# Storing the turned context once and loading it back, in a gated two-layer block on one core

## The reference

```
x = x + tanh(g_xattn[0]) * L0_xattn(layernorm(x), ctx, ctx, Wq, bq, ...)
x = x + tanh(g_ffn[0])   * L0_ffn(layernorm(x), controller, f1, f2, bias)
x = x + tanh(g_xattn[1]) * L1_xattn(layernorm(x), ctx, ctx, mask)
x = x + tanh(g_ffn[1])   * L1_ffn(layernorm(x), ln_g, ln_b, w1, w2)
# L0_xattn: 16 heads of 32; a query sees itself and every 32nd key
#   k = ctx @ Wk + bk; v = ctx @ Wv + bv; q = x @ Wq + bq; softmax(q k^T / sqrt(32)) v @ Wo + bo
# L0_ffn: in each group of 16 tokens, 64 slots each pick the token with the
#   largest logit; relu(sel @ f1 + bias) @ f2 is added back to the picked token
# L1_xattn: one head of width 512, no projections
logits = einsum('bqd,bkd->bqk', q, k) * 512**-0.5 + mask * -1e9
out    = einsum('bqk,bkd->bqd', softmax(logits), v)        # k = v = ctx
# L1_ffn: layernorm, int8 activations (scale from a 0.995 quantile), ternary weights, gelu
```

## Time and profile before

| | |
|---|---|
| median of three runs | 2006.31 us (2002.03 to 2006.43) |
| profiled execution | 2007.47 us, its span 2005.9 us |
| busy of the span | PE 1554.9, DVE 1184.0, PEld 1038.0, ACT 900.8, POOL 413.3 us |
| first stage, `phase1` | 23 to 662 us |
| `phase2a` | 663.6 to 873.1 us |
| joint stage, `phase2b3` | 873.9 to 1348.1 us |
| rest | 1349.2 us to the end |
| DMA | 167.08 MB, 83 GB/s over the span |

### The profile page before, as it was taken

One profiled execution on the slowest core, in us unless ns is written; L12 is line 12 of the kernel. 1 busy time (PEld: TensorE's weight loads), 2 busy tenths in 40 slices (PEclk: granted clock), 3 DMA queues, 4 the chain that ended last, 5 costly groups with the idle time before them and its releaser, 6 DMA issues. The chain is left out here.

```text
span 2005.9 us, 30396 instructions
## 1 busy us (share of the span) xinstructions
PE 1554.9 (78%) x10558; PEld 1038.0 (52%) x10558; DVE 1184.0 (59%) x2707; ACT 900.8 (45%) x1582; POOL 413.3 (21%) x411
## 2 busy tenths in 40 slices
PE   3999999999996488838999999931145991299996
PEld 3777767777774477714555555531133441134442
DVE  4576676666664344303676666755665896555552
ACT  2333333323322255523555555533066663477772
POOL 0232232232232100011455554450000000000000
PEclk9999999999998699968999999975566995599998
DMA  4112212211211832264233333218000000012221
GB/s 150 64 55 75 86 54 75 85 54 75 85 39 54 282 115 95 85 215 141 90 111 111 99 110 111 80 64 326 0 2 2 1 0 2 0 43 85 84 84 45
DMA packets 80829, 167.08 MB, mean 83 GB/s; under 512 B 14064, under 2 KB 25680, under 8 KB 79696
## 3 DMA queue, kind: packets, MB, share of 16 engines
q1 hardware_dynamic: 76304, 148.90, 21.3%
q0 software_dynamic: 4416, 16.78, 2.5%
HBM read 110.34 MB, written 55.31 MB: 83 GB/s over the span
## 5 line engine op out<-in xcount | busy, mean ns | idle before, releaser
L1892 PE MATMUL p_z<-qT,w1T 128*128 (+1 forms) x1024 | 246.8, 386 | 8.5 <-PEq L113 6.0
L1892 PEld LDWEIGHTS p_z<-qT,w1T 128*128 128x128 bf16 x1024 | 100.5, 99 | 137.1 <-issue 14.5
L1378 DVE TENSOR_TENSOR p_il<-p_f,p_ih 128x512 fp32r<-128x512 f32 x128 | 88.5, 692 | 129.6 <-ACT p_ih L1214 129.1
L1214 ACT ACTIVATE p_ih<-p_f 128x512 fp32r<-128x512 f32 x128 | 76.5, 598 | 152.5 <-PE p_f L1090 152.5
L1090 PE MATMUL p_f<-p_f2s,p_z 128*32 128x512 f32 x1024 | 137.6, 611 | 1.0 <-DMA p_z<-inner_d 0.6
L2202 PE MATMUL p_o<-w2T,p_Gq 128*128 128x512 bf16 x512 | 128.7, 381 | 2.2 <-DVE p_Gq L2270 2.2
L943 DVE COPY p_selT<-p_sel 128x512 f32<-128x512 f32 x64 | 66.8, 1046 | 96.0 <-PE p_sel L850 96.0
L850 PE MATMUL p_sel<-p_pick,p_xp 128*128 128x128 bf16 (+1 forms) x1536 | 97.2, 229 | 31.9 <-ACT p_selT L899 18.7
L2288 DVE TENSOR_SCALAR p_r<-p_g,p_s 128x512 f32<-128x512 f32 x128 | 62.2, 486 | 90.7 <-ACT p_g L2228 90.6
L850 PEld LDWEIGHTS p_sel<-p_pick,p_xp 128*128 128x128 bf16 x1536 | 94.0, 103 | 38.1 <-issue 29.7
L1949 DVE MAX8 p_tops<-hid 128x8 f32<-128x128 f32 x512 | 99.6, 278 | 23.0 <-ACT hid L1933 23.0
(11 more groups left out here) (302 smaller groups left out, 4055.3 us busy)
## 6 DMA issues: line engine op xcount, KB each, us to landing
p_cin<-in_ctx_dram SPq DMA_DIRECT2D x32, 512.0 KB, 4.6
xparts<-p_parts SPq DMA_DIRECT2D x16, 768.0 KB, 3.3
p_xp<-xparts SPq DMA_DIRECT2D x4, 3072.0 KB, 24.4
p_xin<-in_x_dram SPq DMA_DIRECT2D x16, 512.0 KB, 4.4
residual<-p_x SPq DMA_DIRECT2D x16, 512.0 KB, 3.2
p_f<-in_L_ffn_f_dram POOLq DMA_DIRECT2D x16, 512.0 KB, 4.3
inner_d<-p_inner POOLq DMA_DIRECT2D x4, 2048.0 KB, 9.4
p_z<-inner_d SPq DMA_DIRECT2D x16, 512.0 KB, 3.7
```

The costliest lines, as they stand in the source:

```text
L1214: act.activation(ih[m % ID][:, :], bf[m % FD][:, :], ACT.Copy).then_inc(s["hi_done"], 1)
L1378: dve.tensor_tensor(il[m % ID][:, :], bf[m % FD][:, :], ih[m % ID][:, :].bitcast(F32), ALU.subtract).then_inc(s["lo_done"], 1)
L1892: mm = pe.matmul(bank, w1T[:, c, fc * P:(fc + 1) * P], qT[:, c, bass.ds(first, TB)], start=(c == 0), stop=(c == C - 1))
```

## The change

The first stage gets a DRAM tensor `ctxT` of 16 batches x 2 parts x 512 KB. In each step SP, after the loads of the next batch, waits for DVE's low part (`ctxT` semaphore), and stores both parts; before ACT writes the buffer again for the next batch it waits for the stores (`ctxT_out`). At the end SP waits for all of them.

In the joint stage `turn_ctx`, the two `turned_highs` and the two `turned_lows` of the context go. POOL issues two loads per batch into the same buffers, after `rstd2` and before `values_low`, once `S_full` says that the scores of the batch before have read them. `scores` waits for `cT_in` in place of `c_low`; `turn_xn` takes over the wait on the bank that `turn_ctx` had; SP's reload of `cin` no longer waits for `cT_full`.

```diff
@@ phase1, block.sync, step @@
                 if F:
+                    sp.wait_ge(s["ctxT"], n.next(s["ctxT"], NT))
+                    n.apart()
+                    for k in range(2):
+                        sp.dma_start(ctxT_d[b, k], ctxT[k][:, :, :].bitcast(F32)).then_inc(s["ctxT_out"], 16)
 
                     sp.wait_ge(s["V_done"], n.next(s["V_done"], NT))
...
             sp.wait_ge(s["perm_out"], 16 * B)
+            sp.wait_ge(s["ctxT_out"], 32 * B)
@@ phase1, block.scalar, step @@
                 if F:
+                    if (used := n.reuse(s["ctxT_out"], 1, 32)) is not None:
+                        act.wait_ge(s["ctxT_out"], used)
                     for t in range(NT):
                         high(ctxT, t, "ctx_high")
@@ phase2b3, block.sync @@
                 if i >= 2 and live(i):
-                    sp.wait_ge(s["cT_full"], NT * (i - 1))
                     sp.wait_ge(s["v_low"], i - 1)
                     load_ctx(i)
@@ phase2b3, block.tensor @@
-            def turn_ctx(b):
-                pe.wait_ge(s[f"c_in{b % 2}"], 16 * (b // 2 + 1))
-                for t in range(NT):
-
-                    if b + 2 < B:
-                        pe.wait_ge(s["permT_done"], NT * (b + 2) + t + 1)
-                    else:
-                        pe.wait_ge(s["n_low"], NT * (b - 1) + t + 1)
-                    turn_tile(bT[t], cin[b % 2][:, t, :], s["cT_full"])
-
             def turn_xn(b):
                 for t in range(NT):
                     pe.wait_ge(s["norm1"], NT * b + t + 1)
-                    pe.wait_ge(s["c_low"], NT * b + t + 1)
+
+                    if b + 2 < B:
+                        pe.wait_ge(s["permT_done"], NT * (b + 2) + t + 1)
+                    elif b >= 1:
+                        pe.wait_ge(s["n_low"], NT * (b - 1) + t + 1)
                     turn_tile(bT[t], xn[:, t, :], s["nT_full"])
 
             def scores(b, t):
                 if t == 0:
-                    pe.wait_ge(s["c_low"], NT * (b + 1))
+                    pe.wait_ge(s["cT_in"], 32 * (b + 1))
                     pe.wait_ge(s["n_low"], NT * (b + 1))
...
-                    if k == 3 and live(i - 1):
-                        turn_ctx(i - 1)
@@ phase2b3, block.scalar @@
-                    if k == 3 and live(i - 1):
-                        turned_highs(i - 1, ctxT, s["cT_full"], s["c_high"])
@@ phase2b3, block.gpsimd @@
+            def load_ctxT(b):
+                if b >= 1:
+                    pool.wait_ge(s["S_full"], b)
+                for k in range(2):
+                    pool.dma_start(ctxT[k][:, :, :], ctxT_d[b, k].bitcast(F32R)).then_inc(s["cT_in"], 16)
...
                 if live(i - 3):
                     rstd2(i - 3)
+                if live(i - 1):
+                    load_ctxT(i - 1)
                 if live(i - 2):
                     values_low(i - 2)
@@ phase2b3, block.vector @@
-                    if k == 4 and live(i - 1):
-                        turned_lows(i - 1, ctxT, s["c_high"], s["c_low"])
```

More of the change, by code:

```diff
@@ L138, in shape_constants, with phase1 @@
     }
-def phase1(nc, x, ctx, gx, Wq, bq, Wk, bk, Wv, bv, Wo, bo, ctrl, K, x_mid, xparts, perm_d, vg_d):
+def phase1(nc, x, ctx, gx, Wq, bq, Wk, bk, Wv, bv, Wo, bo, ctrl, K, x_mid, xparts, perm_d, vg_d, ctxT_d):
     xt = x.rearrange("b (t p) d -> b p t d", p=P)
@@ L257, in phase1 @@
             vg_out vrep_in vbd_done x1_out var2 rstd2 norm2 b0_done r1_done b1_done b2_done parts_out
-            logits_full logits_taken pmT_done aside_sp aside_pe aside_dve""".split()
+            logits_full logits_taken pmT_done ctxT_out aside_sp aside_pe aside_dve""".split()
         s = es.enter_context(semaphores(nc, "p1_", names))
@@ L956, with phase2b3 @@
 NC1 = TILES * D // SEG * 8
-def phase2b3(nc, inner_d, perm_d, f2, gf, x_mid, ctx, mask, gx, ln_g, ln_b, K, x3_d, hid_d, cand):
+def phase2b3(nc, inner_d, perm_d, f2, gf, x_mid, ctx, ctxT_d, mask, gx, ln_g, ln_b, K, x3_d, hid_d, cand):
     FD, ID, ZD, XD, LAG = 2, 3, 2, 4, 2
@@ L996, in phase2b3 @@
         names = """const_in ln_in identb_done tanh_done spread_zero spread_done turned permT_done f_full hi_done lo_done scattered added
-            var1 rstd1 norm1 cT_full c_high c_low nT_full n_high n_low S_full S_taken soft exp e_full e_high e_low rz_done v_high v_low
+            var1 rstd1 norm1 cT_in nT_full n_high n_low S_full S_taken soft exp e_full e_high e_low rz_done v_high v_low
             O_full x3_done var2 rstd2 hh_done hg_done hid_done abs_done max_done own own_pool""".split() + \
@@ L2346, in mk_flamingo_gated @@
     vg_d = dram("global_values", (B, G, D))
+    ctxT_d = dram("ctxT", (B, 2, P, C, S))
     inner_d = dram("inner_d", (P, B, SL // 2, 2, GB // B))
-    phase1(nc, x, ctx, gx, Wq, bq, Wk, bk, Wv, bv, Wo, bo, ctrl, K, x_one, xparts, perm_d, vg_d)
+    phase1(nc, x, ctx, gx, Wq, bq, Wk, bk, Wv, bv, Wo, bo, ctrl, K, x_one, xparts, perm_d, vg_d, ctxT_d)
     phase2a(nc, xparts, perm_d, f1, bias, K, inner_d)
@@ L2352, in mk_flamingo_gated @@
         cand = sbt("cand1", [P, NC1])
-        phase2b3(nc, inner_d, perm_d, f2, gf, x_one, ctx, mask, gx, ln_g, ln_b, K, x_three, hid_d, cand)
+        phase2b3(nc, inner_d, perm_d, f2, gf, x_one, ctx, ctxT_d, mask, gx, ln_g, ln_b, K, x_three, hid_d, cand)
         hid = sbt("hid", [P, TILES, D])
```

## The result

The changed kernel takes 2013.39 us (median of 6 runs, 2011.37 to 2016.23) where the kernel before takes 2006.26 (6 runs, 2002.03 to 2008.36). The ratio is 1.0038 with a 95% interval of 1.0025 to 1.0051: slower, where 1996.8 and faster was forecast. The profiled execution took 2012.82 us, span 2011.3.

A forecast was written before the change was run, and what follows sets the result against it. PE was taken to bound both stages, with ACT's xn chain next. Joint steps gave 7.7 + 0.83 + 0.14 + 0.83 = 9.5 us, so 2007.5 became 1998.0, or 1996.8 on the runs' median; range 1993 to 2000, with rivals 1992.5 to 2003.5.

The forecast's parts named there:

- PE bound, turns worth 0.83 us: Joint stage, step 6: PE busy 25.90 of 26.08 us; removing the context's turns shortens block 3 from 2.95 to 2.12 us.
- The chain to xn is late next, by 0.13 us a step: Joint stage, block 5: ACT's xn allows the scatter at 1060.81, PE alone 1060.68, so step 6 gives 0.70 us.
- What is added in the joint stage costs nothing: POOL's two 512 KB loads per step delay cvl to end near 1049.8; attend needs it at 1058.4, so no cost.
- DVE holding POOL's DMAs, 1.4 us at no cost: Joint stage: DVE's softmax may hold POOL's descriptor writing at each load, 1.4 us in all against 19 us of room.
- rival C: Joint stage: the two loads land late and PE waits at scores every step; 2012 to 2042 us, chance 0.08.
- the bounds: Joint stage: landing of one pair of loads takes between 5 and 21 us, with 5 taken.
- The prediction's other estimate, 3.2 us for one load: Joint stage: landing of one 512 KB load by the skill page's fit for GpSimd's plain DMAs, where the row has 4.3.
- The stores cost nothing: First stage: SP's two 512 KB stores queue nothing and ACT's wait falls in idle time; 0, at most 1.6 us.
- Nothing in the first stage can get faster: First stage, with the added stores: no gain possible; expected as long as before, 639 us.
- Step 16 and the tail at nothing, 1 us either way: End of the joint stage: removed turns only lengthen a 2.64 us idle stretch; 0, with 1 us allowed for PE's clock.

The follow-up runs named there:

- the waiting kernel: The changed kernel, loads still ahead of cvl, with one more POOL wait so that cvl starts after DVE's small sign instruction L1426: 1995.77 us, ratio 0.9953.

## Why the prediction was wrong

Step by step, in the order of the prediction.

- **PE bound, turns worth 0.83 us:** right. Block 3 is 2.12, and with the wait for xn gone too the step is 25.27.
- **The chain to xn is late next, by 0.13 us a step:** right, and it can be read where the lock is gone: with the loads behind cvl block 5 is 4.52 for 4.37, 0.15 us. The step of 25.44 was forecast as 25.4. Up to the last layer that kernel gains 9.1 us against a forecast sum of 9.5. Step by step: 2 gives 0.84 (forecast 0.83), 3 gives 0.08 (0.14), steps 4 to 14 give 0.64 each (0.70), 15 gives 0.82 (0.83). Its time, 1997.07, is near the 1996.8 of the forecast. The sum of the steps was right for a kernel in which cvl stays out of DVE's way. That the totals agree so well is in part luck: its drain is 2.1 us longer than before, and what follows is 2.7 shorter, neither of which is in the sum.
- **What is added in the joint stage costs nothing:** this is the step that failed. The prediction put POOL's two issues ahead of cvl, read its new span as 1047.4 to near 1049.8, and asked of it only when attend needs cvl and who queues behind it on POOL. "None of these is used within 8 us, so all of it costs nothing": it cost a hold of 2.26 us on DVE and 1.19 us of PE in each steady step. Both rows stood side by side: DVE's softmax from 1046.31 is three instructions, the last of them at 1047.75, inside the new span of cvl. What was not asked is which engine runs beside the moved instruction, and whether the two can. The hold was in the trace of the kernel before (866 ns for 169, and 15 times 2.14 us for 0.54 in the first stage) and was not looked for. Nor did the prediction ask what PE did in the 0.18 us of step 6 in which it was not busy. It waited for DVE's additions in block 2, so that beyond 1.06 us of spare each delay on DVE there was one of PE.
- The Trainium skill ("SBUF — State Buffer", section "SBUF: two separate sides") states the rule: VectorE's two-port operations and GpSimd's operations share a port pair, whoever starts first has it for the whole instruction, and the other is fully blocked. The prediction cited that section for DVE holding POOL's DMAs, 1.4 us at no cost, and did not turn it round. The traces agree with the rule for a moved cvl (2.43 us for 0.17). They do not agree on its length: with cvl in halves the hold outlasts one instruction (2.56 us), and the measurement decides. The size could have been had from the rows of the kernel before. By the prediction's own place for cvl, up to 1049.8, L1422 ends 1.9 us later than at 1047.92; less the 0.97 that DVE idled before L1378, that is 0.9 us a step, an estimate, which already takes back all that the turns give. cvl came 0.3 us later than that in its step, and block 2 grew by 1.19. The hold of POOL's issues by DVE that the prediction priced at 1.4 us is not in the trace: they took 0.63 and 0.55 us beside L1421 and L1424, for 0.54. The other way round the runs show 0.10 us on DVE by POOL's DMA issue and no more. Which port mode L1426 runs in, no view shows.
- **The landing of the loads, rival C:** 3.9 and 4.6 us in a steady step, 4.9 and 6.6 with the loads behind cvl. Within the bounds, and PE never waits for them. The prediction's other estimate, 3.2 us for one load, is below all four. That SP can load the same tiles through a float32 view at the same time was not thought of.
- **The stores cost nothing:** right (0.9998, 0.9987 to 1.0009).
- **Nothing in the first stage can get faster:** the joint stage begins 2.2 us sooner in this trace. The stores alone give no gain in the median, so I put this down to the clock stretches; no run shows it by itself.
- **Step 16 and the tail at nothing, 1 us either way:** too narrow. From the last layer to the last attend the changed kernel took 3.7 us more than before.
- **The rivals:** the slower case was named, but by a late landing, 19 us away, while the true one was 0.28 us away at 1047.47. With the price of that collision known (step 26.46, 11 steps of 0.37, and the drain) the sum would have been above 2006.

What stays open: why POOL has the place in every steady step of the changed kernel. The two records start within 0.02 us of each other, POOL's first but for one step (batch 8), in which DVE's starts 0.004 us ahead and is held all the same. At this distance the records do not tell who was first. Both engines start from the same release: POOL's way is 0.63 and 0.55 us of issues after a start at 1045.23, DVE's is 0.69 and 0.69 after 1044.97. That these come to the same moment looks like chance, but no run shifted cvl by a hair to the other side; the waiting kernel parted them by 0.3 us.

Of the 3.7 us of the drain at most 1.5 are the hold. The rest goes with the clock, by three traces. The kernel with the loads behind cvl has no more hold there than the kernel before (0.89 for 0.87 us), and a drain of 33.2 us at a mean clock of 0.73. The kernel in which cvl waits has none, and a drain of 30.6 us at 0.87, near the 31.1 at 0.88 before. So the change does not make the clock fall in each case, and what decides it no run shows.

## What to carry to other kernels

When an instruction of POOL moves in time, look at what DVE does in its new span, and the reverse, even where both have room on their own: a DVE instruction of 0.17 us can cost the whole length of POOL's. In the trace of the kernel before, compare the maximum of a small DVE line with its median; a line of 169/169/866 ns is a collision that has happened once and can happen always, and one of 537/546/2140 has happened in nearly each batch. Then follow the held engine's own queue to what others wait for. Check the releaser that a profile names against the source: here the name was ACT, and the wait was for DVE. The cures are cheap: order, one wait that lets the small one first, a gap between long POOL instructions, or an algebraic fold that removes the small one.

## What the runs showed of the hardware

- A running POOL instruction can hold a DVE instruction to its end: 2.43 us for 0.17 beside a cvl of 2.40, 0.87 where DVE came 1.54 us behind cvl, and 2.14 us for 0.54 beside a product of 2.15 in the first stage (L637).
- The hold covers POOL instructions that follow one another without a wait as one: 2.56 us for two halves of 1.3, 2.57 for a product of 0.23 and cvl of 2.40. A wait of 0.08 us between them ends it.
- It takes only some of DVE's instructions: the sign (128x2) and the normalisation of x (128x512), both TENSOR_SCALAR in and out of the same SBUF tile, are held; the reduction 128x512 to 128x2, and operations that read PSUM, ran in their usual 0.69 us beside POOL. A reciprocal of the same size, also in place (L1441), kept its 0.15 us inside a POOL product of 0.71 us, so size and place alone don't make the hold. Once a TENSOR_TENSOR with both operands in SBUF was held too (L737 of the kernel before, 2.44 us for 0.38).
- Beside POOL's DMA issues of 0.62 and 0.54 us the small instruction took 0.27 us for 0.17.
- Single stretches of 3.4 us at a granted clock of 0.50 fall in the first stage at places that differ from kernel to kernel (one, two or three in its steady part), at 1.6 us each. In the 3.4 us before each of those of the two main traces PE was busy 1.48 to 1.55 us; most waits of that kind had no such stretch behind them. So 2 or 3 us between two single traces say nothing of an edit; the medians of several runs do.
